# A layer of eight experts: rows gathered by a token list instead of scattered, on one core

## The chip, the cores and the metric

The kernel runs on one core of one Trainium2 chip. The metric is the device time of one execution in microseconds (us), the median of several executions. A profile is one further execution, recorded by the hardware profiler.

## The reference

The program is a chain of eight residual layers on `x`, 16 batches of 128 tokens with 256 features. The change touches the feed-forward layers of blocks 0 and 1; the one it rewrites is block 1's, with eight experts:

```
x = x + _L1_ffn_ref(_layernorm(x, axis=-1), Wr, Wg, Wu, Wd)

router_logits = jnp.einsum('bsh,he->bse', hidden_states, Wr)       # 8 experts
topk_logits, selected = jax.lax.top_k(router_logits, 2)
router_probs = jax.nn.softmax(topk_logits, axis=-1)
for e in range(8):
    w_e = jnp.where(selected == e, router_probs, 0.0).sum(axis=-1, keepdims=True)
    g = jnp.clip(jax.nn.silu(hidden_states @ Wg[e]), -7.0, 7.0)
    u = hidden_states @ Wu[e]
    out = out + ((g * u) @ Wd[e]) * w_e
```

Each of the 2048 tokens goes to two experts, so 4096 rows of 256 numbers have to be brought together by expert, multiplied, and brought back.

## The kernel before

The program is a list of stages with a barrier of all five engines between them. Each stage is written by hand, engine by engine, and its engines wait for each other by semaphores. The stages are attention, the layer of 32 experts (`MoeTop6`), the attention with fp8 weights (`Fp8Attention`), the layer of eight experts (`MoeTop2`), and then attention and feed-forward twice more. X, the activations, stays in SBUF throughout.

`MoeTop2` works in three parts.

**Routing** goes over four groups of four batches. On VectorE (DVE) a group has `moments` (mean and variance), `normalise` (writes `n_xn`), `choose` (top two of the eight logits, one-hot rows `n_hot`, running sums `n_before`) and `slots` (from the counts of TensorE, the place of each of a token's two copies). On TensorE (PE) it has `transposes`, `logits` and `counts`. DVE mixes the groups: moments of group g+2 and choose of group g-1 stand between the normalisations, so group 2 is normalised only after group 0 has been chosen. The place is a row of an array in HBM, `top_in`, with a region of 2048 rows for each expert, 16384 rows in all. GpSimd (POOL) scatters: 32 indirect DMAs (L2151), each of 128 rows of 1 KB, at most eight in flight. `top_in` is set to zero beforehand by eight DMAs of 2 MB each (`clear`, L1776), which SP issues in the middle of the stage before. After the fourth group `layout` works out, for each of the 39 tiles of 128 rows that the experts can fill together, whose expert it is (`n_own`) and which rows of `top_in` it has (`n_row`).

**The expert loop** takes the 39 tiles. POOL gathers a tile's rows (L2161, after all scatters have landed, six tiles ahead), PE transposes them (`rows_T`, L1864), multiplies by Wg and Wu (`up`, L1877), transposes the hidden rows (L1889) and multiplies by Wd (`down`, L1900). SP stores each result tile to `top_out`. `places`, in the second step of the loop on DVE, works out where in `top_out` a token's two rows will be.

**Return**: when all result tiles are stored, POOL gathers two rows for each token (32 indirect DMAs) and DVE adds them to X.

SP loads constants and all expert weights (16 DMAs, 6.3 MB) at the start of the stage, and `up` waits for all of them before the first tile.

`MoeTop6` already has a token list: `places` writes two arrays of ones in bf16, `m_in_tile` (which tile a copy is in, times the token's batch, and times its lane) and `m_at_place` (which of the 128 rows of the tile); PE multiplies one by the other (`tokens`, L1320), which sums up to "the token at each place"; after a transpose `end_tokens` makes `m_token`, and POOL gathers from `moe_in`, the normalised tokens in their own order (L1706). `m_at_place` is made by 24 instructions of 128x128 for each group:

```
for n in range(NG * TOP_K):
    i, j = divmod(n, TOP_K)
    x = v.tensor_scalar(self.at_place[:, i, j, :], self.count16[:, :], self.cutf[:, 1, i, j:j + 1], None, ALU.is_equal)
```

## Time and profile before

| | |
|---|---|
| median of 3 executions | 2559.22 us (2554.13 to 2559.9) |
| profiled execution, its own time | 2561.87 us |
| span of the profiled execution | 2560.1 us |
| mean granted TensorE clock | 0.877 of full |
| PE, DVE, ACT, POOL busy | 2031.7, 1799.2, 1404.7, 1214.1 us |

The span runs from the first to the last instruction. Starts are us from the span's start. In a timeline row the columns are the start, the length, the engine, the line of the kernel, the operation, what it writes and reads, how many instructions are merged, and in brackets how long the engine stood idle before and what ended that. A granted clock of 1.00 is 2.4 GHz, and 0.50 is 1.2 GHz. In a row of windows the pairs are the busy us and the count of PE, PEld (weight loads), DVE, ACT and POOL, followed by the granted clock, the busy share of the DMA engines and GB/s.

### The profile page before, as it was taken

The page shows a single profiled execution, that of the slowest core. Times are in us where ns is not written, and L with a number is a line of the kernel's source. Part 1 is how long each engine was busy: PE and PEld are TensorE (multiplying, and loading weights), DVE is VectorE, ACT ScalarE, POOL GpSimd, SP SyncE. Part 2 cuts the span into 40 slices and gives each one's busy share as a digit, 9 for nine tenths or more (in the row PEclk, how much of TensorE's full clock was granted, in tenths as well). Part 3 has the DMA queues.
Part 4 walks back from the last instruction along what each step waited for, and adds up shares of the span by engine and source line. Part 5 has one row for each costly group of instructions (what it writes and reads, how often), then busy time and mean ns, then how long its engine had stood idle before and what let it go on. Part 6 is the DMA issues. An engine that isn't in the chain of part 4 may idle for free. (4 is left out here: it accounts for less than half of the span.)

```text
span 2560.1 us, 42709 instructions
## 1 busy us (share of the span) xinstructions
PE 2031.7 (79%) x13434; PEld 1241.5 (48%) x13434; DVE 1799.2 (70%) x4099; ACT 1404.7 (55%) x3553; POOL 1214.1 (47%) x1425
## 2 busy tenths in 40 slices
PE   6999699996899999999999539708844536787487
PEld 3444356663577767677777426404412223333144
DVE  4899594755798999999997623338837756888254
ACT  1777322541788888888888403205644422677343
POOL 4443003435788888888876363265412212343100
PEclk9999789997999999999999759857876655999599
DMA  4566305772207000000000222259710015676100
GB/s 134 168 173 170 119 1 156 243 241 62 44 20 284 20 18 20 23 16 20 20 9 1 101 87 88 75 167 237 205 60 1 1 49 145 160 189 176 44 1 33
DMA packets 264488, 242.06 MB, mean 95 GB/s; under 512 B 37002, under 2 KB 236141, under 8 KB 263629
## 3 DMA queue, kind: packets, MB, share of 16 engines
q1 hardware_dynamic: 237996, 187.71, 25.2%
q0 software_dynamic: 13776, 36.59, 5.2%
q10 hardware_dynamic: 12496, 15.03, 1.7%
q8 instruction: 114, 1.87, 0.3%
q14 instruction: 106, 0.86, 0.1%
HBM read 141.95 MB, written 98.19 MB: 94 GB/s over the span
## 5 line engine op out<-in xcount | busy, mean ns | idle before, releaser
L736 DVE TENSOR_REDUCE a_nm<-bank 128x2 f32<-128x512 f32 x640 | 408.8, 683 | 36.8 <-PE bank L602 34.6
L844 ACT ACTIVATE a_PT<-bank 128x512 f32<-128x512 f32 x640 | 355.4, 603 | 142.9 <-PE bank L609 128.1
L602 PE MATMUL bank<-a_stack_k,a_stack_q 48*128 48x256 bf16 (+2 forms) x1280 | 262.1, 298 | 99.1 <-DVE a_nm L736 61.1
L2858 PE MATMUL bank<-f_w,f_zc 128*128 128x512 bf16 x1152 | 283.6, 383 | 22.3 <-DVE f_zc L2966 18.1
L3178 POOL TENSOR_TENSOR f_hr<-f_hr,half_pow 128x4 f32<-128x4 f32 x192 | 245.4, 1278 | 85.2 <-DVE f_hr L2975 85.1
L609 PE MATMUL bank<-a_stack_q,a_stack_k 51*128 51x256 bf16 (+2 forms) x1280 | 251.2, 288 | 7.6 <-ACT a_PT L844 7.1
L3070 ACT ACTIVATE f_Pm<-bank,f_nmax 128x128 f32<-128x128 f32 x512 | 182.5, 382 | 73.6 <-DVE f_nmax L2990 72.9
L602 PEld LDWEIGHTS bank<-a_stack_k,a_stack_q 48*128 48x128 bf16 (+2 forms) x1280 | 91.6, 99 | 261.5 <-DVE a_nm L736 179.5
L624 PE MATMUL bank<-a_PT,a_V 128*32 128x256 f32 x2560 | 186.2, 412 | 1.4 <-ACT a_PT L844 1.4
L2858 PEld LDWEIGHTS bank<-f_w,f_zc 128*128 128x128 bf16 x1152 | 112.5, 99 | 122.5 <-issue 25.8
L3167 POOL TENSOR_TENSOR f_cf<-f_cbr,f_cmr 128x516 f32<-128x516 bf16 x128 | 156.9, 1226 | 12.6 <-DVE f_cb L3015 11.0
L2985 DVE TENSOR_TENSOR f_raw<-bank,f_hr 128x512 f32<-128x512 f32 x192 | 131.5, 685 | 42.9 <-POOL f_hr L3178 42.8
L1706 POOL DMA_INDIRECT m_xe<-moe_in,m_token x64 | 75.8, 1184 | 178.6 <-DVE m_token L1584 93.8
L3082 ACT ACTIVATE f_cb<-bank,f_rsmooth 128x128 bf16<-128x128 f32 x512 | 147.1, 377 | 23.8 <-PE bank L2818 23.8
L2975 DVE TENSOR_REDUCE f_hr<-f_sq 128x4 f32<-128x516 f32 x192 | 131.3, 684 | 39.2 <-ACT f_sq L3105 37.2
L3105 ACT ACTIVATE f_sq<-bank 128x512 f32<-128x512 f32 x192 | 116.5, 607 | 62.7 <-PE bank L2858 39.3
L3172 POOL TENSOR_TENSOR f_Pm<-f_Pm,f_rs 128x512 f32<-128x512 f32 x128 | 132.6, 1036 | 23.3 <-DVE f_rs L2995 23.1
L2807 PEld LDWEIGHTS bank<-f_KT,f_QT 128*128 128x128 f32 x1024 | 129.3, 192 | 20.0 <-issue 10.8
L2807 PE MATMUL bank<-f_KT,f_QT 128*128 128x128 f32 x1024 | 135.2, 275 | 0.0
L2818 PE MATMUL bank<-f_PT,f_Vv 128*128 128x256 f32 x512 | 132.1, 381 | 2.3 <-ACT f_cb L3082 2.3
L930 POOL TENSOR_TENSOR a_rest<-a_QK,a_parts 128x512 f32<-128x512 f32 x48 | 55.7, 1161 | 164.0 <-ACT a_parts L901 164.0
L977 POOL DMA_INDIRECT f_rows<-moe_out,slot x96 | 107.5, 1120 | 46.1 <-ACTq L129 29.8
(365 smaller groups left out, 4804.1 us busy)
## 6 DMA issues: line engine op xcount, KB each, us to landing
cut<-a_parts SPq DMA_DIRECT2D x96, 192.0 KB
cut<-a_parts SPq DMA_DIRECT2D x144, 128.0 KB
o<-a_O SPq DMA_DIRECT2D x32, 512.0 KB, 3.7
top_in<-zero SPq DMA_DIRECT2D x8, 2048.0 KB, 19.4
a_stack_q<-cut SPq DMA_DIRECT2D x64, 192.0 KB
a_stack_k<-cut SPq DMA_DIRECT2D x64, 192.0 KB
m_w<-in_w SPq DMA_DIRECT2D x32, 368.0 KB
moe_out<-m_oe ACTq DMA_DIRECT2D x32, 256.0 KB
```

Source lines behind the costliest of these rows:

```text
L602: x = t.matmul(ps[:, n * D:(n + 1) * D], self.stack_q[rows, i, slot, n * P:(n + 1) * P], self.stack_k[rows, i, slot, :], start=True, stop= ...
L609: x = t.matmul(ps[:, n * D:(n + 1) * D], self.stack_k[rows, i, slot, n * P:(n + 1) * P], self.stack_q[rows, i, slot, :], start=True, stop= ...
L624: x = t.matmul(self.k.bank[6][32 * s:32 * s + 32, half], self.V1[:, b % self.NV, m, first + s, :], self.PT[:, (4 * q + s) % 8, m, :], star ...
L736: v.tensor_reduce(self.nm[:, g % 2, :, at % self.J, at // self.J], self.k.bank[h % 3][:, :].rearrange("p (n m) -> p n m", n=2), AX.X, ALU. ...
L844: a.activation(self.PT[:, h % 8, :, :].rearrange("p m n -> p (m n)"), self.k.bank[3 + h % 3][:, :], ACT.Exp).then_inc(self.a_exp.sem, 1)
L2807: x = t.matmul(ps[:, j * P:(j + 1) * P], self.QT[:, cross, h, :], self.KT[:, cross, h // 2, :], start=True, stop=True)
L2858: x = t.matmul(ps[:, :], self.zc[:, b % 2, j, c_, :], self.fp8.w3[:, m, c_, at:at + BANK], start=(m == 0 and c_ == 0), stop=(m == 2 and c_ ...
L3070: x = a.activation(self.Pm[:, i, j * P:(j + 1) * P], ps[:, j * P:(j + 1) * P], ACT.Exp, bias=self.nmax[:, i, j:j + 1], accum_out=self.rs[: ...
L3082: x = a.activation(self.cb[:, u % self.NCB, j * P:(j + 1) * P], ps[:, j * P:(j + 1) * P], ACT.Copy, scale=self.fp8.rsmooth[:, h:h + 1])
L3167: g.tensor_tensor(self.cf[:, :].rearrange("p (r n) -> p r n", r=3), clipped, steps, ALU.add).then_inc(self.g_c.sem, 1)
L3172: g.tensor_tensor(pm, pm, self.rs[:, u % 3, :].unsqueeze(2).to_broadcast([P, self.HPB, P]), ALU.mult).then_inc(self.g_P.sem, 1)
L3178: g.tensor_tensor(f, f, self.k.half_pow[:, 0:self.HPB], ALU.pow).then_inc(self.g_hr.sem, 1)
```

## The change

`MoeTop2` no longer scatters. The normalised tokens are written to `moe_in` by four plain DMAs. `slots` also writes `n_at_place` for its group; after the fourth group a new function, `list_tokens`, writes `n_in_tile`; PE multiplies (32 products of ones, 78 columns by 128), DVE copies, PE transposes, DVE copies again and makes `n_token`; POOL's 39 gathers take their rows from `moe_in`. `clear`, `top_in`, `n_row` and the 32 scatters are gone. All groups are normalised before the first is chosen. SP stores the tokens between the weights of experts 0 to 3 and those of 4 to 7. In `MoeTop6` the 24 instructions for `m_at_place` become one.

```diff
 class MoeTop6(Stage):            # places()
-        for n in range(NG * TOP_K):
-            i, j = divmod(n, TOP_K)
-            x = v.tensor_scalar(self.at_place[:, i, j, :], self.count16[:, :], self.cutf[:, 1, i, j:j + 1], None, ALU.is_equal)
-            if n < NG * TOP_K - 1:
-                c.mark(x)
-        x.then_inc(self.v_hot.sem, 1)
+        v.tensor_tensor(self.at_place[:, :, :, :], counting(P), self.spread(self.cutf[:, 1, :, :], P), ALU.is_equal).then_inc(self.v_hot.sem, 1)
 class MoeTop2(Stage):            # sp()
-        sp.dma_start(self.tile[:, :, :], A["c_tile"]).then_inc(self.d_par.sem, 16)
+        sp.dma_start(self.count[:, :], A["c_count"]).then_inc(self.d_par.sem, 16)
+        sp.dma_start(self.lane[:, :], A["c_lane"]).then_inc(self.d_par.sem, 16)
+        self.load_experts(sp, range(0, 4))
+        for g in range(self.GROUPS):
+            bs = slice(self.NG * g, self.NG * (g + 1))
+            sp.wait_ge(self.v_n.sem, self.v_n.at(g + 1))
+            sp.dma_start(self.rows_in[:, bs, :], self.xn[:, bs, :]).then_inc(self.d_rows.sem, 16)
+        self.load_experts(sp, range(4, self.NE))
                                  # pe()
-        for g in range(self.GROUPS + 2):
+        for g in range(self.GROUPS + 3):
             if g < self.GROUPS:
                 self.transposes(t, g)
             if 1 <= g <= self.GROUPS:
                 self.logits(t, g - 1)
-            if g >= 2:
-                self.counts(t, g - 2)
+            if g >= 3:
+                self.counts(t, g - 3)
         self.totals(t)
+        self.tokens(t)
+    def tokens(self, t):
+        n, last = 2 * self.NT, 2 * B - 1
+        t.wait_ge(self.v_hot.sem, self.v_hot.at(1))
+        for i in range(2 * B):
+            b, j = divmod(i, 2)
+            x = t.matmul(self.k.bank[7][0:n, 0:P], self.in_tile[:, b, j, :, :].rearrange("p m n -> p (m n)"), self.at_place[:, b, j, :],
+                         start=(i == 0), stop=(i == last))
+        x.then_inc(self.p_who.sem, 1)
+        t.wait_ge(self.v_who.sem, self.v_who.at(1))
+        t.transpose(self.k.bank[6][:, 0:n], self.who[:, :], self.k.ident[0:n, 0:n]).then_inc(self.p_list.sem, 1)
                                  # dve()
-        self.moments(v, 0)
-        self.moments(v, 1)
-        self.constants(v)
-        for g in range(self.GROUPS + 2):
+        for g in range(self.GROUPS + 1):
             if g < self.GROUPS:
-                self.normalise(v, g)
-            if g + 2 < self.GROUPS:
-                self.moments(v, g + 2)
-            if 1 <= g <= self.GROUPS:
-                self.choose(v, g - 1)
-            if g >= 2:
-                self.slots(v, g - 2)
-        self.layout(v)
+                self.moments(v, g)
+            if g == 1:
+                self.constants(v)
+            if g:
+                self.normalise(v, g - 1)
+        for g in range(self.GROUPS + 1):
+            if g < self.GROUPS:
+                self.choose(v, g)
+            if g == self.GROUPS:
+                self.layout(v)
+            if g:
+                self.slots(v, g - 1)
+        self.list_tokens(v)
                                  # slots(), at its end
+        v.wait_ge(self.v_slot.sem, self.v_slot.at(g + 1))
+        c.mark(v.tensor_scalar(self.cut[:, 0, sl, :], self.slot[:, sl, :], 7, None, ALU.logical_shift_right))
+        c.mark(v.tensor_scalar(self.cut[:, 1, sl, :], self.slot[:, sl, :], P - 1, None, ALU.bitwise_and))
+        c.after()
+        c.mark(v.tensor_copy(self.cutf[:, :, sl, :], self.cut[:, :, sl, :]))
+        c.after()
+        c.mark(v.tensor_tensor(self.at_place[:, sl, :, :], self.counting(NG, 2, P), self.spread(self.cutf[:, 1, sl, :], P), ALU.is_equal))
+    def list_tokens(self, v):
+        c.after()
+        self.by_expert(v, slice(0, B), self.tiles[:, 1, :].unsqueeze(1).to_broadcast([P, B, self.NE]))
+        c.mark(v.tensor_tensor(self.cutf[:, 0, :, :], self.cutf[:, 0, :, :], self.slotf[:, :, :], ALU.add))
+        c.after()
+        c.mark(v.tensor_tensor(tile[:, :, :, 0, :], self.counting(B, 2, NT), self.spread(self.cutf[:, 0, :, :], NT), ALU.is_equal))
+        c.after()
+        c.mark(v.tensor_tensor(tile[:, :, :, 1, :], tile[:, :, :, 0, :],
+                               self.spread(self.spread(self.count[:, 0:B], 2), NT), ALU.mult))
+        c.after()
+        v.tensor_scalar(tile[:, :, :, 0, :], tile[:, :, :, 0, :], self.lane[:, 0:1], None, ALU.mult).then_inc(self.v_hot.sem, 1)
+        self.owners(v)
+        v.wait_ge(self.p_who.sem, self.p_who.at(1))
+        v.tensor_copy(self.who[:, :], self.k.bank[7][0:2 * NT, 0:P]).then_inc(self.v_who.sem, 1)
+        v.wait_ge(self.p_list.sem, self.p_list.at(1))
+        v.tensor_copy(self.listed[:, :, :].rearrange("p m n -> p (m n)"), self.k.bank[6][:, 0:2 * NT]).then_inc(self.v_list.sem, 1)
+        v.wait_ge(self.v_list.sem, self.v_list.at(1))
+        v.scalar_tensor_tensor(self.token[:, :], self.listed[:, 1, :], float(P), self.listed[:, 0, :], ALU.mult,
+                               ALU.add).then_inc(self.v_token.sem, 1)
                                  # pool()
-        g.wait_ge(self.d_clear.sem, self.d_clear.at(self.NE))
-        for b in range(B):
-            ...
-                g.indirect_dma_start(self.rows_in, at, self.xn[:, b, :], None, bounds_check=self.NE * self.REGION - 1,
-                                     oob_is_err=False).then_inc(self.d_scat[b % 4].sem, 16)
-        g.wait_ge(self.v_row.sem, self.v_row.at(1))
-        for i in range(4):
-            g.wait_ge(self.d_scat[i].sem, self.d_scat[i].at(2 * (B // 4)))
+        g.wait_ge(self.v_token.sem, self.v_token.at(1))
+        g.wait_ge(self.d_rows.sem, self.d_rows.at(self.GROUPS))
 class Fp8Attention(Stage):       # sp()
-            if b == 4 and self.top2:
-                self.top2.clear(sp)
```

On DVE, from the end of the routing of `MoeTop2`, the kernel before has this (the names are the arrays named above; `n_past` and `n_rowf` lead to `n_row`):

```order
L2018 TENSOR_SCALAR n_tiles<-bank 128x8
L2020 TENSOR_SCALAR n_tiles<-n_tiles 128x8
L2022 TENSOR_TENSOR n_upto<-n_upto,n_tiles 128x64
L2023 TENSOR_SCALAR n_tiles<-n_tiles 128x8
L2025 TENSOR_REDUCE n_incl<-n_upto 128x8
L2027 TENSOR_TENSOR n_past<-n_incl,n_tile 128x273
L2030 TENSOR_REDUCE n_ownf<-n_past 1x39
L2031 TENSOR_TENSOR n_pastw<-n_past,n_tiles 128x273
L2034 CAST n_own<-n_ownf 1x39
L2035 TENSOR_REDUCE n_rowf<-n_pastw 128x39
L2037 TENSOR_TENSOR n_rowf<-n_rowf,n_tile 128x39
L2039 TENSOR_SCALAR n_row<-n_rowf 128x39
```

The changed kernel has, at the same place, from the last instruction of the fourth group's `slots` on (`n_cutf` holds tile and place of each copy as numbers):

```order
L2028 TENSOR_TENSOR n_at_place<-n_count,n_cutf 128x1024
L2008 TENSOR_TENSOR n_hotw<-n_hot,n_tiles 128x16x8 x2
L2010 TENSOR_REDUCE n_slotf<-n_hotw 128x32
L2060 TENSOR_TENSOR n_cutf<-n_cutf,n_slotf 128x32
L2062 TENSOR_TENSOR n_in_tile<-n_count,n_cutf 128x32x39
L2064 TENSOR_TENSOR n_in_tile<-n_in_tile,n_count 128x32x39
L2067 TENSOR_SCALAR n_in_tile<-n_in_tile,n_lane 128x32x39
L2080 TENSOR_TENSOR n_past<-n_incl,n_count 1x273
L2083 TENSOR_REDUCE n_ownf<-n_past 1x39
L2085 CAST n_own<-n_ownf 1x39
L2070 COPY n_who<-bank 78x128
L2074 SCALAR_TENSOR_TENSOR n_token<-n_listed 128x39
```

The owners of the tiles now come after the arrays of ones, and the chain from there to the list runs over PE and back twice (of the last rows, the copy to `n_listed` is left out).

On PE, the routing of `MoeTop2` before, from its first transposes to the total counts:

```order
L1827 MATMUL bank<-ident,n_xn 128x128 x16
L1837 MATMUL bank<-n_wr,n_xnT 128x8 x8
L1827 MATMUL bank<-ident,n_xn 128x128 x8
L1837 MATMUL bank<-n_wr,n_xnT 128x8 x8
L1850 MATMUL bank<-n_before,n_ones 128x32
L1851 MATMUL bank<-n_hit,n_tri 128x32
L1827 MATMUL bank<-ident,n_xn 128x128 x8
L1837 MATMUL bank<-n_wr,n_xnT 128x8 x8
```

And the changed one, over the same work and its new end:

```order
L1833 MATMUL bank<-n_wr,n_xnT 128x8 x8
L1823 MATMUL bank<-ident,n_xn 128x128 x8
L1833 MATMUL bank<-n_wr,n_xnT 128x8 x8
L1846 MATMUL bank<-n_before,n_ones 128x32
L1847 MATMUL bank<-n_hit,n_tri 128x32
L1833 MATMUL bank<-n_wr,n_xnT 128x8 x8
```

The first counts (`n_before`, `n_hit`) moved behind the last transposes, that is, one group later than before.

## Rows read from the trace of the kernel before

**Rows 1.** Timeline of POOL in `MoeTop2`: first scatter, last scatter, first gather

```profile
1474.72 1.07 POOL L2151 DMA_INDIRECT top_in<-n_xn,n_slot  x1 [16.52 <-DVE n_slot L2011]
...
1515.80 0.97 POOL L2151 DMA_INDIRECT top_in<-n_xn,n_slot  x1 [0.30 <-DMA top_in<-n_xn,n_slot]
1519.05 1.04 POOL L2161 DMA_INDIRECT n_xe<-top_in,n_row  x1 [2.28 <-DMA top_in<-n_xn,n_slot]
```

**Rows 2.** Windows in `MoeTop2`: two of the routing, one of the expert loop

```profile
1460.00:1465.00 5.00, 0.66 (x3) 0.56 (x4) 3.94 (x26) 0.20 (x1) 0.00 (x0) 0.50 1.01 391
1465.00:1470.00 5.00, 5.00 (x26) 4.90 (x25) 0.03 (x1) 1.17 (x2) 0.00 (x0) 0.50 0.01 4
...
1600.00:1640.00 40.00, 40.00 (x161) 24.87 (x160) 13.96 (x41) 13.79 (x41) 6.98 (x7) 1.00 0.23 70
```

**Rows 3.** Timeline of DVE at the start of `MoeTop2`

```profile
1445.78 1.41 DVE L1934 BATCH_NORM_STATS2 n_stats<-X 128x6 f32<-128x256 f32 x4 [5.35 <-POOLq L129]
...
1450.08 0.23 DVE L1946 CAST n_tri<-n_trif 128x128 bf16<-128x128 f32 x1 [0.35 <-DMA n_tile<-in_c_tile]
...
1450.58 1.38 DVE L1957 TENSOR_SCALAR n_xn<-X,n_mv,n_rstd 128x256 f32<-128x256 f32 x4
...
1453.80 1.38 DVE L1957 TENSOR_SCALAR n_xn<-X,n_mv,n_rstd 128x256 f32<-128x256 f32 x4
```

**Rows 4.** Timeline of PE: transposes of group 1, logits of group 0

```profile
1455.23 1.97 PE L1827 MATMUL bank<-ident,n_xn 128*128 128x128 f32 x8 [1.19 <-DVE n_xn L1957]
...
1456.99 3.42 PE L1837 MATMUL bank<-n_wr,n_xnT 128*128 128x8 f32 x16
```

**Rows 5.** Timeline of DVE: `choose` of group 1, `slots` of group 0, next

```profile
1469.97 0.19 DVE L1969 COPY n_lg<-bank 128x32 f32<-128x32 f32 x1 [5.28 <-PE bank L1837]
...
1472.84 0.19 DVE L2007 TENSOR_TENSOR n_where<-bank,n_region 128x32 f32<-128x32 f32 x1
...
1473.72 1.38 DVE L1957 TENSOR_SCALAR n_xn<-X,n_mv,n_rstd 128x256 f32<-128x256 f32 x4
```

**Rows 6.** Timeline of DVE in `MoeTop6`: the arrays of ones, fourth group

```profile
384.19 1.76 DVE L1555 TENSOR_TENSOR m_in_tile<-m_count,m_cutf 128x1536 bf16<-128x1536 f32 x1
...
386.79 0.62 DVE L1560 TENSOR_SCALAR m_in_tile<-m_in_tile,m_lane 128x1536 bf16<-128x1536 bf16 x1
387.32 3.99 DVE L1563 TENSOR_SCALAR m_at_place<-m_count,m_cutf 128x128 bf16<-128x128 bf16 x24
```

**Rows 7.** Timeline of DVE in the expert loop: `places` over all batches

```profile
1530.16 0.49 DVE L1999 TENSOR_TENSOR n_hotw<-n_hot,n_where 128x128 f32<-128x128 f32 x2
...
1530.69 0.42 DVE L2001 TENSOR_REDUCE n_slotf<-n_hotw 128x32 f32<-128x256 f32 x1
```

**Rows 8.** Timeline of `MoeTop6`: products of ones, token list, first gather

```profile
394.89 1.50 PE L1320 MATMUL bank<-m_at_place,m_in_tile 128*128 128x128 bf16 x24
...
400.87 0.23 DVE L1584 SCALAR_TENSOR_TENSOR m_token<-m_who 128x64 uint32<-128x64 f32 x1
402.00 1.22 POOL L1706 DMA_INDIRECT m_xe<-moe_in,m_token  x1 [93.78 <-DVE m_token L1584]
```

**Rows 9.** Timeline of PE at the start of the expert loop

```profile
1521.98 0.66 PE L1864 MATMUL bank<-ident,n_xe 128*128 128x128 f32 x2 [32.03 <-issue]
...
1524.34 3.78 PE L1877 MATMUL bank<-n_wgu,n_xeT 128*128 x4 [0.39 <-issue]
```

**Rows 10.** Instructions of `clear`: min/median/max ns, first and last start

```profile
L1776 SPq DMA_DIRECT2D top_in<-zero x8: 592/4989/5706, 785.6 to 812.4; - x8
```

**Rows 11.** Timeline of ACT in `Fp8Attention`: one copy in each batch

```profile
776.45 0.41 ACT L3055 COPY f_zT<-bank 128x256 f32<-128x256 f32 x1
...
826.49 0.42 ACT L3055 COPY f_zT<-bank 128x256 f32<-128x256 f32 x1
...
876.52 0.41 ACT L3055 COPY f_zT<-bank 128x256 f32<-128x256 f32 x1
```

**Rows 12.** Waits of PE in `MoeTop6`'s routing: us, times, longest

```profile
PE bank L1302 <- DVE m_hit L1516: 4.8, 3, 1.8
```

More of the change, by code:

```diff
@@ L1753, in signals @@
         claim, G, NT = self.k.sig.claim, self.GROUPS, self.NT
-        self.d_par, self.d_w = claim("d_par", 4, 16), claim("n_d_w", 2 * self.NE, 16)
-        self.d_scat = [claim(f"n_d_scat{i}", B // 4 * 2, 16, own=True) for i in range(4)]
+        self.d_par, self.d_w = claim("d_par", 5, 16), claim("n_d_w", 2 * self.NE, 16)
+        self.d_rows = claim("n_d_rows", G, 16)
         self.d_xe = [claim(f"n_d_xe{i}", -(-(NT - i) // self.RX), 16, own=True) for i in range(self.RX)]
@@ L1767, in signals @@
         self.v_sum = claim("n_v_sum", B)
-    def clear(self, sp):
-        k, n = self.k, 8
-        rows = self.rows_in.rearrange("(e p n r) d -> e p n (r d)", e=self.NE, p=P, n=n)
-        for e in range(self.NE):
-            sp.dma_start(rows[e], k.zero[:, :].unsqueeze(1).to_broadcast([P, n, FILL])).then_inc(self.d_clear.sem, 16)
     def sp(self, sp):
@@ L2022, in layout @@
         c.mark(v.tensor_tensor(self.upto[:, :, :], self.upto[:, :, :], n.unsqueeze(1).to_broadcast([P, NE, NE]), ALU.mult))
-        c.mark(v.tensor_scalar(tiles[:, 1, :], n, -float(P), float(self.REGION), ALU.mult, ALU.add))
         c.after()
@@ L2026, in layout @@
         c.after()
-        c.mark(v.tensor_tensor(self.past[:, :, :], self.incl[:, 0:NE - 1].unsqueeze(1).to_broadcast([P, NT, NE - 1]),
-                               self.tile[:, 0, :].unsqueeze(2).to_broadcast([P, NT, NE - 1]), ALU.is_le))
+        c.mark(v.tensor_tensor(before, self.incl[:, :], n, ALU.subtract))
+    def list_tokens(self, v):
+        c, NT, tile = self.k.dve, self.NT, self.in_tile
+        flat = lambda a: a.rearrange("p b j -> p (b j)")
         c.after()
-        c.mark(v.tensor_reduce(self.ownf[:, :], self.past[0:1, :, :], AX.X, ALU.add))
@@ L2033, in layout @@
         c.after()
         v.tensor_copy(self.own[:, :], self.ownf[:, :]).then_inc(self.v_own.sem, 1)
-        c.mark(v.tensor_reduce(self.rowf[:, :], self.pastw[:, :, :], AX.X, ALU.add))
-        c.after()
-        c.mark(v.tensor_tensor(self.rowf[:, :], self.rowf[:, :], self.tile[:, 1, :], ALU.add))
-        c.after()
-        v.tensor_scalar(self.row[:, :], self.rowf[:, :], float(NE * self.REGION - 1), None, ALU.min).then_inc(self.v_row.sem, 1)
-    def places(self, v):
-        c, NE, pr = self.k.dve, self.NE, self.pr
-        before = self.tiles[:, 2, :]
-        c.mark(v.tensor_tensor(before, self.incl[:, :], self.tiles[:, 0, :], ALU.subtract))
-        c.after()
-        c.mark(v.scalar_tensor_tensor(before, before, float(P), self.region[:, 0, :], ALU.mult, ALU.subtract))
-        c.after()
-        c.mark(v.tensor_scalar(before, before, -1.0, None, ALU.add))
-        c.after()
-        c.mark(v.tensor_tensor(self.where[:, :, :], self.where[:, :, :], before.unsqueeze(1).to_broadcast([P, B, NE]), ALU.add))
-        c.after()
-        self.by_expert(v, slice(0, B), self.where[:, :, :])
-        v.tensor_copy(self.place[:, :, :], self.slotf[:, :, :]).then_inc(self.v_place.sem, 1)
@@ L2055, in places @@
+    def places(self, v):
+        c, pr = self.k.dve, self.pr
+        v.scalar_tensor_tensor(self.place[:, :, :], self.cutf[:, 0, :, :], float(P), self.cutf[:, 1, :, :], ALU.mult,
+                               ALU.add).then_inc(self.v_place.sem, 1)
         v.wait_ge(self.a_df.sem, self.a_df.at(self.GROUPS))
@@ L3195, in program @@
             stage(Attention(k, 0, None))
-        top2 = MoeTop2(k, 1 not in stages) if 3 in stages else None
         if 1 in stages:
@@ L3202, in program @@
                 stage(MoeTop6(k, combine, fp8))
-                stage(Fp8Attention(k, combine, fp8, top2))
+                stage(Fp8Attention(k, combine, fp8))
         if 3 in stages:
-            stage(top2)
+            stage(MoeTop2(k))
         if 4 in stages:
```

90 lines of the change are left out of this document (46 added, 44 removed).

## The prediction

> **What bounds the kernel now.** The change lies in three stages, so I read those stages and not the whole. First the timeline of POOL in the stage of eight experts. Its scatters run from 1474.72 to 1515.80 us, 32 of them, 1.33 us apart, each about 1.0 us of work for POOL; the first gather starts at 1519.05, held at the end by the landing of the last scatter [rows 1]. Then the windows: in the routing TensorE's granted clock is 0.50 even where it is busy for 5.00 of 5.00 us; in the expert loop TensorE is busy for 40.00 of 40.00 us at full clock, so the loop is TensorE's own time [rows 2]. From this, everything between the start of the stage (1445.78) and the first gather (1519.05) is time in which the loop waits, 73.3 us, and for the last 44.3 of them it is POOL alone that counts. What the change is worth is the start of the first gather, before against after. The timelines of VectorE and TensorE in the routing give the pieces for that [rows 3 to 5]. The list itself is shown by its twin, the layer of 32 experts, in timelines [rows 6, 8].
>
> **The new path to the first gather.** I walk it from 1445.78, with the durations of the kernel before.
>
> *Normalisation.* Two moments, a wait for constants and the small constants take 4.80 us, to 1450.58 [rows 3]. There was a wait of 0.35 us for the last constant. Now one more tiny constant is issued behind a slightly larger one; I add 0.4 us, bounded by 0 and 1. The first normalisation starts at 1451.0. A normalisation and a moment together took 3.22 us (1450.58 to 1453.80) [rows 3], so the second starts at 1454.2. The last two groups follow by about 1460.2; they are hidden, since TensorE is now behind.
>
> *TensorE.* Its transposes of group 1 started 1.43 us after the normalisation of that group did, and the logits of group 0 ended 5.18 us after those transposes started (1455.23 to 1456.99 + 3.42) [rows 4]. So now: transposes at 1455.6, logits 0 done at 1460.8, and with 5.18 us for each further pair of transposes and logits, logits 1 at 1466.0 and logits 2 at 1471.2. The first counts stand behind these and are done at 1471.5. This is the price of normalising all groups first: the first place is known later. Nothing waits for it alone any more.
>
> *VectorE.* One `choose` is 2.87 us (1469.97 to 1472.84), one `slots` 0.88 us (1472.84 to 1473.72) [rows 5]. `slots` grows by two cuts and a cast (0.5 us) and by the array of ones, 1024 elements. The twin writes 1536 elements of the same form in 1.76 us [rows 6]; with about 0.16 us that do not scale, 1024 are 1.23 us. A `slots` is then 2.65 us. Chooses 0 and 1 are done while TensorE works on; from 1471.5 VectorE alone sets the pace: four `slots` (10.6), two `choose` (5.7), the shortened `layout` (five small instructions, 1.0): 1488.8.
>
> *List.* `n_hotw` and its reduction over all batches took 0.98 us with their waits (0.49 and 0.42 busy) [rows 7], the sum 0.2. Two arrays of 1248 elements at the twin's rate are 1.46 each, 3.0 with the waits; the last, single-source one is 0.55 (0.62 for 1536 elements [rows 6]). Together 4.8 us: 1493.6. TensorE's 32 products follow: 24 took 1.50 us [rows 8] at full clock, so 2.0, and at half clock 4.0. The clock stood at 0.50 in this routing [rows 2]; I take 4.0. The owners of the tiles are made meanwhile. Copy, transpose, copy: 1.3 us, sized by the small instructions around. The token instruction starts at 1499.0, and the twin's first gather started 1.13 us after it (400.87 to 402.00) [rows 8]. First gather: 1500.2.
>
> That is **18.9 us** earlier than 1519.05. I round the path up by 0.3 for gaps that I haven't counted: 18.6.
>
> **What else moves.** *Expert weights.* Half of them now wait on SP behind the four stores of tokens, which wait for the normalisations, so they go out from about 1460.2. With the stores (2.1 MB) 5.2 MB remain; at the 391 GB/s of [rows 2] that takes 13.4 us, to 1474. The first tile needs them near 1503, so they cost nothing; that cover ends only below 121 GB/s. Before, the queue was empty again from 1465 on (4 GB/s) [rows 2]. The stores have landed long before the gather that needs them.
>
> *The clearing.* Its eight DMAs run from 785.6 to 812.4 [rows 10]. The batch of the fp8 attention in which they fall lasts 50.04 us (776.45 to 826.49), the next one, without them, 50.03 [rows 11]. So taking them away gains nothing.
>
> *The layer of 32 experts.* 24 instructions, 3.99 us, become one of 3072 elements: by the row of 1536 that is 1.60 x 2 + 0.16 = 3.36 us, 0.63 less [rows 6]. TensorE waits for VectorE's `m_hit` three times, the longest 1.8 us [rows 12]; two of these waits have a `places` ahead of them in VectorE's order (those of groups 1 and 2); the `places` of groups 0 and 3 lie where TensorE is behind. So twice 0.63, 1.3 us with the dropped cast, bounds 0 and 4.7 (a re-rise of the clock after each wait could go too, about 1.7 us each, by the 3.78 against half of it for the same four products in [rows 9]). Here the Trainium skill speaks against the change: "VectorE: DVE Perf Modes", section "The TRN2 errata", gives a fixed 58 cycles and one element a cycle for an instruction with two tensors, four for a single-source one in bf16. By its figures 24 small ones would be 2.25 us (an estimate) and the big one 3.26, a loss of 1.0 for each group and 2.0 on the path; this trace has 3.99 for the 24, so it doesn't agree.
>
> *The rest.* The expert loop has the same products, the 32 gathers at the end and their places are the same, the later stages are untouched.
>
> **Sum.** 2561.87 (the profiled execution's own time) - 18.6 - 1.3 = 2542.0. The median of the timed runs is 2.65 below the profiled one, so the prediction is **2539.3 us**, 0.78% less.
>
> **The rivals.**
> - *The clock rises in the routing (faster than forecast).* TensorE is now busy without a gap from 1455.6 to 1471.5, and it could be granted 2.4 GHz; the pairs of 5.18 us would shrink, until VectorE sets the pace from about 1465.9 (end of the last normalisation plus two `choose`), and the products of ones would take 2.0: up to 7.6 us, 2532. Against it: the window with 5.00 of 5.00 busy at 0.50 [rows 2]. A smaller form of it is the start of the loop, where the first products took 3.78 us, cold [rows 9]; up to 3 us less if the products of ones warm the array. Chance 12%. The Trainium skill, "TensorE: Matmul & The Clock Gate", section "What's actually happening", says that a busy array is passed every clock pulse; by that rule alone this rival would be the forecast, and the trace of this routing doesn't bear it out.
> - *The chain is longer (smaller gain).* VectorE, TensorE, VectorE, TensorE, VectorE, POOL hand over to each other, and each gap may be larger; or the constants are late. Twice my allowances is 5 us: 2544. Chance 10%.
> - *The weights are late.* Below 121 GB/s `up` would wait. At 80 GB/s they would land at 1525 and all is lost again: 2558, no change. Against it: 391 GB/s [rows 2]. 2%.
> - *The gathers are slow (slower than before).* Rows now lie scattered in `moe_in`, and all of the 896 empty places (39 x 128 - 4096) read the same row, where a tile used to read consecutive rows. The loop turns in about 3.06 us (40 us for some 13 tiles) [rows 2]. If a gather took more than that, all 39 would hold the loop: at 3.54 us the gain is gone, at 3.8 the kernel is 10 us slower, 2568. For it: nothing in the trace shows such a gather with many equal rows. Against it: the twin gathers from the same array. 3%.
> - *No gain to see* for a reason I don't know, 3%.
>
> **How the numbers follow.** The forecast itself has 70%; its own terms give 2535 to 2544: the clock in the products of ones (-2), the constants (-0.4 to +0.6), `MoeTop6` (-3.4 to +1.3), gaps (+2), and the repetition of the median (its three runs lie 5.8 us apart). The range takes in most of the first two rivals: 2532 to 2546. A measurement of this kernel can tell about 0.3%, 7.7 us, from no change. Faster takes the forecast, the first two rivals and a part of the last: 0.94; no change 0.03; slower 0.03.
>
> **What the changed kernel's profile would show.** First gather near 1499 (that is 1500.2 less the 1.3 us of the earlier stage), right behind `n_token`; first counts near 1470; VectorE dense from there to about 1492; 32 products in 4 us at clock 0.50; TensorE waiting for no weights; the batches of the fp8 attention still 50.04 us; loop and return as long as before. I am wrong if the first gather stands after 1504 or before 1495, or if the loop has become longer than before.

## The result, and the profile after

The changed kernel takes **2530.9 us** (median of 4 executions, 2527.77 to 2534.57), the kernel before 2557.16 us beside it on the same chip (2554.13 to 2559.9). The ratio is 0.9898, interval 0.9876 to 0.9920, which is 26.1 us less (26.3 by the two medians), between 20.5 and 31.7. The prediction was 2539.3, range 2532 to 2546: the direction is right, the gain is larger than the range allows, by 1.1 us. The profiled execution of the changed kernel took 2534.57 us, with a span of 2532.8 and a mean granted clock of 0.883.

DVE at the start of `MoeTop2` (answers to [rows 3]; columns as there):

```profile
1449.22 1.41 DVE L1944 BATCH_NORM_STATS2 n_stats<-X 128x6 f32<-128x256 f32 x4 [5.35 <-POOLq L129]
...
1453.09 0.23 DVE L1956 CAST n_tri<-n_trif 128x128 bf16<-128x128 f32 x1
...
1453.52 1.37 DVE L1966 TENSOR_SCALAR n_xn<-X,n_mv,n_rstd 128x256 f32<-128x256 f32 x4
```

All times of the routing are best read from the stage's first instruction, 1449.22 now and 1445.78 before. The wait for constants has gone altogether: the first normalisation starts 4.30 us into the stage, where it was 4.80 us.

PE from the second transposes to the loop (answers to [rows 4, 8 and 9]):

```profile
1458.16 1.97 PE L1823 MATMUL bank<-ident,n_xn 128*128 128x128 f32 x8 [1.19 <-DVE n_xn L1966]
1459.92 3.42 PE L1833 MATMUL bank<-n_wr,n_xnT 128*128 128x8 f32 x16
1463.20 1.95 PE L1823 MATMUL bank<-ident,n_xn 128*128 128x128 f32 x8
1464.94 3.42 PE L1833 MATMUL bank<-n_wr,n_xnT 128*128 128x8 f32 x16
1468.21 1.95 PE L1823 MATMUL bank<-ident,n_xn 128*128 128x128 f32 x8
1469.95 3.42 PE L1833 MATMUL bank<-n_wr,n_xnT 128*128 128x8 f32 x16
1473.22 0.19 PE L1846 MATMUL bank<-n_before,n_ones 128*128 128x32 bf16 x1
...
1495.76 3.63 PE L1858 MATMUL bank<-n_at_place,n_in_tile 128*78 128x128 bf16 x32 [10.95 <-DVE n_in_tile L2067]
1499.77 0.39 PE L1862 MATMUL bank<-ident,n_who 78*128 78x78 f32 x1 [0.38 <-DVE n_who L2070]
1504.40 0.66 PE L1872 MATMUL bank<-ident,n_xe 128*128 128x128 f32 x2 [4.23 <-issue]
```

TensorE now works without a gap from 1458.16 through the counts of the first two groups, to 1476.91; from there it waits for VectorE, the last time for 10.95 us. VectorE over the same stretch (answers to [rows 5 to 8]):

```profile
1473.55 0.19 DVE L2017 TENSOR_SCALAR n_where<-bank 128x32 f32<-128x32 f32 x1 [2.25 <-PE bank L1847]
...
1475.05 1.23 DVE L2028 TENSOR_TENSOR n_at_place<-n_count,n_cutf 128x1024 bf16<-128x1024 f32 x1
1476.19 0.18 DVE L1978 COPY n_lg<-bank 128x32 f32<-128x32 f32 x1
...
1492.15 1.46 DVE L2062 TENSOR_TENSOR n_in_tile<-n_count,n_cutf 128x1248 bf16<-128x1248 f32 x1
1493.65 1.46 DVE L2064 TENSOR_TENSOR n_in_tile<-n_in_tile,n_count 128x1248 bf16<-128x1248 bf16 x1
1495.14 0.56 DVE L2067 TENSOR_SCALAR n_in_tile<-n_in_tile,n_lane 128x1248 bf16<-128x1248 bf16 x1
...
1500.47 0.20 DVE L2074 SCALAR_TENSOR_TENSOR n_token<-n_listed 128x39 uint32<-128x39 f32 x1
```

Between 1473.55 and 1495.70 VectorE has no idle time in brackets: it is the bound of this stretch. The gather follows. POOL's timeline (the first line answers to [rows 1]; the last two are the end of the stage and its barrier):

```profile
1501.46 1.09 POOL L2187 DMA_INDIRECT n_xe<-moe_in,n_token  x1 [40.10 <-DVE n_token L2074]
...
1670.66 1.00 POOL L2198 DMA_INDIRECT n_rows<-top_out,n_place  x1 [0.30 <-issue]
1677.61 0.52 POOL L906 MEMSET a_V<- 128x512 f32 x1 [5.96 <-POOLq L129]
```

The first gather comes 52.2 us into the stage, where it was 73.3. The last line is one that I had not looked at before: POOL's first instruction of the next stage, with 5.96 us from the last gather to it, and `POOLq L129`, POOL's own drain and barrier, as what it waited for. In POOL's timeline of the kernel before the same place reads:

```profile
1689.19 1.00 POOL L2172 DMA_INDIRECT n_rows<-top_out,n_place  x1 [0.31 <-issue]
1698.76 0.52 POOL L908 MEMSET a_V<- 128x512 f32 x1 [8.57 <-POOLq L129]
```

VectorE's last addition ends 2.8 us after that gather does, in both. Behind it VectorE waits for POOL; its first instruction of the next stage, in the kernel before and then in the changed one:

```profile
1698.76 0.27 DVE L698 MEMSET a_one<- 3x256 bf16 x1 [5.75 <-POOLq L129]
```

```profile
1677.61 0.27 DVE L696 MEMSET a_one<- 3x256 bf16 x1 [3.15 <-POOLq L129]
```

How the gain runs through the program, by the first (or last) start of an instruction in each of the two profiles (the differences are taken before rounding):

| from ... to | before | after | |
|---|---|---|---|
| start to `m_stats` (attention 0) | 297.7 | 303.8 | +6.2 |
| to `m_token` (routing of `MoeTop6`) | 103.2 | 100.4 | -2.8 |
| to `n_stats` (experts, fp8 attention) | 1044.9 | 1044.9 | 0 |
| to first `n_xe` gather (routing of `MoeTop2`) | 73.3 | 52.2 | -21.0 |
| to first `n_rows` gather (expert loop) | 129.5 | 128.8 | -0.7 |
| to last `n_rows` gather (return) | 40.6 | 40.4 | -0.2 |
| to `b_stats` (barrier, attention 2) | 206.3 | 203.3 | -2.9 |
| to last `a_stats` (block 2's feed-forward, most of attention 3) | 433.2 | 431.7 | -1.6 |
| to `t_stats` (end of attention 3) | 81.1 | 77.2 | -3.9 |
| to the end | 150.3 | 150.0 | -0.3 |

Steps that contain no changed instruction moved by up to 6 us too; in this pair their shifts nearly cancel. How much of each shift is the change could not be told from one pair, and that is what most of the experiments are for.

### The profile page after: what moved, and what is told of

It is laid out like the page before. It is cut to its first block and busy times, and to the rows that moved or that the text cites. A ratio compares the mean times of both kernels' runs of the same rounds, so it can differ in the third digit from the quotient of the medians.

```text
span 2532.8 us, 42624 instructions
## 1 busy us (share of the span) xinstructions
PE 2033.0 (80%) x13467; PEld 1245.5 (49%) x13467; DVE 1807.1 (71%) x4020; ACT 1404.6 (55%) x3553; POOL 1182.0 (47%) x1393
```

## The experiments

Each run leaves a profile too, so every kernel is one more sample of all the stages that it doesn't touch. "Stage" below is the time from `n_stats` to the first gather.

**Theory A**: the gain is what the two changed places give, and the rest is variation between executions. **Rival B**: removing 16 MB of `top_in` and its clearing made later stages faster.

### The list without the one large instruction

```diff
 # MoeTop6.places()
-        v.tensor_tensor(self.at_place[:, :, :, :], counting(P), self.spread(self.cutf[:, 1, :, :], P), ALU.is_equal)...
+        for n in range(NG * TOP_K):
+            ...
+            x = v.tensor_scalar(self.at_place[:, i, j, :], self.count16[:, :], self.cutf[:, 1, i, j:j + 1], None, ALU.is_equal)
```

> The changed kernel with the 24 small instructions for m_at_place put back in MoeTop6; everything else as changed. Theory A (what the change saves lies in two places: 21.0 us from the start of the eight-expert stage to its first gather, and about 2.7 us in the routing of MoeTop6; the few us by which untouched attention stages moved, +6.1 and about -9, are a variation between executions): from the start of MoeTop2 to its first gather 52.2 us as in the changed kernel; m_stats to m_token back at 103.2 us from 100.5; gain over the kernel before 21 to 23 us in the median. Rival B (the stages behind MoeTop2 really became faster because 16 MB of top_in, and its clearing, are gone): a_stats to t_stats and the step before b_stats are shorter than in the kernel before by 3 to 4 us each here too.

Measured: 2532.14 us against 2559.42, ratio 0.9898 (0.9877 to 0.9919). The stage is 52.4 us, as theory A has it. `m_stats` to `m_token` is 105.1, not less than the 103.2 expected, and the gain in the median is 27.3 us where 21 to 23 was expected: the number was missed, and without the large instruction the kernel is not measurably slower. Rival B isn't settled here: the steps that it names are 202.5 (to `b_stats`) and 77.2 us (to `t_stats`), shorter than before by as much as it says.

### The one large instruction alone

```diff
 # the kernel before, MoeTop6.places()
-        for n in range(NG * TOP_K): ...
+        v.tensor_tensor(self.at_place[:, :, :, :], counting(P), self.spread(self.cutf[:, 1, :, :], P), ALU.is_equal)...
```

> The kernel before with only the one large instruction for m_at_place in MoeTop6. By the prediction's term it gains 1.3 us; by what the changed kernel's trace suggests 2.7, because TensorE's granted clock does not fall after its second wait for m_hit: in the trace m_stats to m_token would be 100.5 us, not 103.2 (or 101.9 if only the durations count). The median can hardly tell either from nothing. Rival C (a loss: one element after another in one large instruction is slower than 24 small ones): 105 us. Theory A also expects here, in attention stages whose code is that of the kernel before, shifts of several us of either sign against the first profile.

Measured: 2557.4 us (12 executions) against 2559.42 (17), ratio 1.0000 (0.9988 to 1.0013). `m_stats` to `m_token` is 100.5. Rival C's 105 us stands in none of the twelve profiles with the large instruction: they give that step as 100.4 or 100.5 three times and 102.3 to 103.5 nine times (mean 102.4). The two without it have 103.2 and 105.1, a difference of 1.8 us on average; but 103.2 lies among the nine, so from two profiles the size can't be told. Where the 2.8 of the first pair has its luck, the windows show. In the three short ones (the changed kernel, this one, and the one with 32 gathers below) TensorE's granted clock stays at 1.00 from 345 us to the list; in the nine others it falls to 0.50 for some 3 to 7 us about TensorE's last wait for `m_hit`, and the list comes 13.5 us after the start of the last array and not 12.2.

This run also answers the question on the untouched stages. Behind `m_token` it is the kernel before, instruction for instruction, yet its `m_stats` stands at 305.2 (the kernel before: 297.7) and its last `a_stats` to `t_stats` is 77.0 (the kernel before: 81.1). Over all fourteen profiles `m_stats` lies between 296.8 and 305.4, and that last step between 75.8 and 81.1, on both sides of the change. Theory A holds for them. This run also has 72.3 us from `n_stats` to the first gather, with the routing of the kernel before, whose profile has 73.3: a stage can differ by 1 us without a change.

### The clearing kept

```diff
 # Fp8Attention.sp()
+            if b == 4 and self.top2:
+                self.top2.clear(sp)          # 8 x 2 MB into an array that nobody reads
 # MoeTop2.pool()
+        g.wait_ge(self.d_clear.sem, self.d_clear.at(self.NE))
```

> The changed kernel with the 16 MB array in HBM and its eight clearing DMAs in the middle of the fp8 attention kept (nothing reads the array; the gathers wait for the clearing too). Theory A: same time as the changed kernel within its scatter, 2528 to 2534, and batches of the fp8 attention of 50.04 us with and without the clearing; a step from MoeTop2's last add to b_stats and from a_stats to t_stats that varies as in the others. Rival B: those two steps go back to the lengths before (202.9 and 81.1 us), about 7 us slower, 2536 to 2540.

Measured: 2529.87 us against 2559.42, ratio 0.9885 (0.9865 to 0.9906), so not slower than the changed kernel; last `n_rows` to `b_stats` is 200.5, shorter than in the changed kernel, and last `a_stats` to `t_stats` 80.1, which two kernels without the clearing have as well (80.4 and 80.2). Rival B is refuted, and the prediction's zero for the clearing stands.

### The old order of the groups, with the list

```diff
 # MoeTop2.dve(); PE's counts of group g-2 likewise
-        for g in range(self.GROUPS + 1): moments(g); normalise(g - 1)
-        for g in range(self.GROUPS + 1): choose(g); slots(g - 1)
+        for g in range(self.GROUPS + 2): normalise(g); moments(g + 2); choose(g - 1); slots(g - 2)
```

> The changed kernel with the groups mixed on VectorE as before (normalisation of group g, moments of g+2, choice of g-1, slots of g-2) and counts of group g-2 on TensorE; the token list is kept. Theory A (the order is worth something because TensorE at half clock would otherwise wait for each normalisation): last choice near 41 + 2 us after the start of the stage, then two slots, layout and the list: first gather 60 to 64 us after the stage's start against 52.2, 8 to 11 us slower than the changed kernel. Rival D (the order is worth nothing, the list alone brings the gain, since VectorE's sum of work is the same): 52 to 54 us.

Measured: 2537.93 us against 2559.42, ratio 0.9914 (0.9892 to 0.9935). Stage 61.0, as theory A has it; rival D is refuted. The median is 7.0 us above that of the changed kernel. VectorE's timeline shows where it goes, the start of `choose` for the second and third groups:

```profile
1472.77 0.19 DVE L1978 COPY n_lg<-bank 128x32 f32<-128x32 f32 x1 [5.27 <-PE bank L1833]
...
1484.92 0.19 DVE L1978 COPY n_lg<-bank 128x32 f32<-128x32 f32 x1 [5.27 <-PE bank L1833]
```

Each time a group's normalisation stands behind the `choose` of an earlier group, TensorE gets it late and VectorE then waits 5.27 us for the logits. With the 3.34 us in front of the first `choose` these waits add up to 13.9 us. With all groups normalised first there are three of 0.60, 2.25 and 2.25 us (in front of the first and second `choose` and the first `slots`), 5.1 together: that is the 8.8 us less. Of the 21.0 us of the stage, the order with its later counts is 8.7 and the list 12.3 (73.3 to 61.0).

### Three edits to the new routing

First, counts of a group one step earlier on TensorE:

```diff
 # MoeTop2.pe()
-            if g >= 3:
-                self.counts(t, g - 3)
+            if g >= 2:
+                self.counts(t, g - 2)
```

> The changed kernel with one edit on TensorE: the counts of group g stand right behind the logits of group g+1 and not of g+2. The prediction said that VectorE alone sets the pace from the first counts on, and VectorE idles 2.25 us in front of the first place computation. Theory A: this idle time goes, first gather 50.0 us after the start of the stage against 52.3, 2.3 us faster. Rival: TensorE then waits for VectorE's choice and its transposes of group 3 and logits come later: no gain, 52.3.

Measured: 2526.54 us against 2558.87, ratio 0.9882 (0.9860 to 0.9904). Stage 50.0: the idle time of 2.25 us in front of the first `slots` is gone. The first counts did have something waiting for them alone, and the new order doesn't need them late: with the counts where the old order has them, the order is worth 11.0 us (61.0 to 50.0).

Second, the last array in two halves:

```diff
 # MoeTop2.list_tokens()
-        (three instructions on n_in_tile, all 16 batches)
+        for h in range(2):
+            bs = slice(h * B // 2, (h + 1) * B // 2)
+            (the same three on batches bs)  ... .then_inc(self.v_hot.sem, 1)
```

> The changed kernel with n_in_tile written for batches 0 to 7 first and 8 to 15 behind, and the 32 products of ones begun after the first half. The 32 products took 3.63 us with the clock at 0.50, all behind the last instruction on n_in_tile. If they cost their full length on the path, half of them (1.8 us) now lies beside VectorE's second half, less 0.4 us for three more small instructions: first gather 50.9 us after the stage's start against 52.3. If the products slow VectorE down or wait for something else, 52.3 or more.

PE begins its products after the first half. Measured: 2532.91 us against 2558.87, ratio 0.9889 (0.9869 to 0.9909). Stage 50.9, as expected; VectorE's wait for the products falls from 2.72 to 0.97 us.

Third, TensorE is kept busy while it waits, with products whose result nobody reads:

```diff
 # MoeTop2.pe()
         self.totals(t)
+        self.idle_products(t, 20)
         self.tokens(t)
+        self.idle_products(t, 8)
```

> The changed kernel with idle products (128x512, bf16, result unused) on TensorE: 20 of them while it waits for the list (where it stood idle for 10.95 us), 8 while it waits for the first gather. If the granted clock follows what TensorE does, the products of ones run at 1.00 in 1.8 us and not 3.63, and the loop starts at full clock, where it now runs at 0.50 for some 9.6 us (1504.40 to about 1514): 4 to 6 us faster in all. Rival: the clock stays at 0.50 in the routing whatever TensorE does (it did where it was busy for 5.00 of 5.00 us), no gain, or a loss of 1 us where the idle products stand in the way.

Measured: 2529.09 us against 2558.87, ratio 0.9897 (0.9866 to 0.9929). Stage 51.8 us, loop 129.5. The granted clock in windows over the idle products, the gap behind them, the products of ones and the loop's start (last three figures: granted clock, DMA share, GB/s):

```profile
1479.00:1482.00 3.00, 3.00 (x9) 1.07 (x8) 2.73 (x10) 0.00 (x0) 0.00 (x0) 0.50 0.00 0
1482.00:1485.00 3.00, 2.80 (x13) 1.07 (x11) 2.75 (x11) 0.00 (x0) 0.00 (x0) 0.98 0.00 0
1485.00:1488.00 3.00, 0.00 (x0) 0.00 (x0) 2.86 (x6) 0.00 (x0) 0.00 (x0) 1.00 0.00 0
1488.00:1491.00 3.00, 1.34 (x13) 1.34 (x14) 2.51 (x5) 0.00 (x0) 0.00 (x0) 0.66 0.00 0
1491.00:1494.00 3.00, 2.62 (x26) 2.19 (x25) 0.62 (x3) 0.00 (x0) 0.00 (x0) 0.77 0.00 0
...
1500.00:1503.00 3.00, 2.73 (x4) 1.19 (x5) 0.00 (x0) 1.54 (x2) 2.19 (x3) 0.50 0.31 87
```

Neither side was right as it stood. The clock does rise with what TensorE does (0.98 at the end of the idle products), so 0.50 is no law of this routing. But the idle products were then done (at 1484.8, 4.9 us before the last array of ones was), the clock fell again just before the products of ones began (0.50 from 1489; 3.26 us for them, not 1.8), and at the loop's first `up` it was back at 0.50. So 0.5 us was gained in the stage and 0.7 given back in the loop, whose clock came back 11 us after the first gather and not 10 (windows of 1 us: 1506 after 1494.90, in the changed kernel 1511 after 1501.46). That also says that the expected 4 to 6 us were too many: the loop of the changed kernel ran at 0.50 until 1511, 6.7 us from its first transposes, not 9.6. A longer row of idle products was not tried.

### What the barrier costs

Scatters put back, beside the loop:

```diff
 # MoeTop2.pool(), behind the gather of tile j, n = j - 6, n = 0 to 31
+                at = bass.IndirectOffsetOnAxis(ap=self.place[:, n // 2, n % 2:n % 2 + 1], axis=0)
+                g.indirect_dma_start(self.spare, at, self.xn[:, n // 2, :], None, ...)
```

> The changed kernel with 32 indirect scatters more: POOL writes the normalised rows into an array that nobody reads, one behind each of the gathers 6 to 37, beside the expert loop. It asks about the barrier behind MoeTop2: POOL needed 8.57 us from its last gather to the next stage in both kernels with scatters and 5.96 us in all four with the list (VectorE waited 5.75 and 3.15 us for it). Theory E (the drain of POOL costs more after more indirect DMAs or after scatters): 8.57 us again here. Rival F (it is about where POOL's program lies, or what is gone from the stages before): 5.96 or another number. It also says whether scatters are dear by themselves: the loop is TensorE's own time, so 128.7 us from first gather to first return gather if they are free beside it.

Measured: 2531.57 us against 2558.87, ratio 0.9903 (0.9877 to 0.9929). The loop is 128.7, the barrier:

```profile
1679.62 0.52 POOL L906 MEMSET a_V<- 128x512 f32 x1 [8.57 <-POOLq L129]
```

8.57 us, the number of the kernel before to the hundredth, as theory E has it, and VectorE's wait is 5.74. The median can't show these 2.6 us: it is 0.7 above that of the changed kernel, and its four executions lie 11 us apart. Three more kernels, with a single execution each, ask what exactly is counted. POOL with 96 small instructions more:

```diff
+        for n in range(96):
+            g.memset(self.idle[:, n, :], 0.0)
```

> The changed kernel with 96 tiny memsets more on POOL, while POOL waits for the list. Asks about the barrier behind MoeTop2, which cost 5.96 us with the list and 8.57 us when 32 scatters were put back beside the loop. If the number of POOL's instructions in the stage counts: about 8.6 or more. If it is the indirect DMAs: 5.96.

32 gathers in place of the 32 scatters:

```diff
-                g.indirect_dma_start(self.spare, at, self.xn[:, n // 2, :], None, ...)
+                g.indirect_dma_start(self.unused[:, n % 4, :], None, self.k.xbuf, at, ...)
```

> The changed kernel with 32 more indirect gathers beside the loop (into a tile that nobody reads), where the earlier run had 32 scatters. If the barrier grows with the number of indirect DMAs of either kind: 8.57 us. If only scatters (rows written to HBM by POOL) make it dearer: 5.96.

16 scatters in place of 32:

```diff
-            if 0 <= n < 2 * B:
+            if 0 <= n < B:
```

> The changed kernel with 16 more scatters beside the loop, half of those of the earlier run. If the barrier grows by a fixed price for each indirect DMA (2.61 us for 32, 0.082 each): 7.27 us. If it is a step (one scatter is enough, or a threshold): 5.96 or 8.57.

POOL's first instruction behind the barrier, small instructions:

```profile
1672.82 0.53 POOL L906 MEMSET a_V<- 128x512 f32 x1 [5.96 <-POOLq L129]
```

32 gathers:

```profile
1689.24 0.53 POOL L906 MEMSET a_V<- 128x512 f32 x1 [8.57 <-POOLq L129]
```

16 scatters:

```profile
1685.06 0.53 POOL L906 MEMSET a_V<- 128x512 f32 x1 [7.26 <-POOLq L129]
```

So it is the number of indirect DMAs that the stage has issued on POOL, scatters and gathers alike: 71 give 5.96, 87 give 7.26, 103 give 8.57, which is 0.082 us each, and by that line some 0.17 us would be left for none (5.96 - 71 x 0.0816, an estimate). The traces bear that out: in the stages that issue no indirect DMA, POOL's drain ends 0.07 to 0.08 us after POOL's last work. POOL's other instructions don't count. Each of these DMAs moves 128 rows, so a price for each row can't be told from a price for each DMA.

The three times were 2526.68, 2539.64 and 2539.91 us. In the last two the loop took 136.1 and 134.1 us, where 32 scatters left it at 128.7; PE's waits there add up to about 4 us more, 2.4 of them in one place. Why they did and the 32 scatters didn't stays open; more DMAs alone is no explanation, since 16 of them were slower than 32.

### Both edits to the routing together

> The changed kernel with both edits that shortened the routing: counts one group earlier (2.3 us) and n_in_tile in two halves (1.4 us). They lie one behind the other on the path, so they should add: first gather 48.6 us after the stage's start against 52.3, and 3.7 us less than the changed kernel in all. If one hid what the other takes away: 49.5 to 50.0.

Measured: 2528.53 us (5 executions) against 2557.95, ratio 0.9886 (0.9865 to 0.9906). Stage 48.8: the two edits add (2.2 and 1.3 alone, 3.4 together). This is the shortest stage of all the kernels, and its profiled execution, 2525.56 us, is the lowest of the profiled ones. The medians can't tell it from the changed kernel.

## Why the prediction was right in direction and short in size

Against 2539.3 the measured median is 8.4 us lower. Of that, 2.1 is luck of the measurement: the median of the kernel before was 2557.2 beside the changed kernel and not 2559.2. The rest is in four places. None of them shows in the prediction's own signs of being wrong: counted from the stage's start in the kernel before, less the 1.3 us, the first gather stands at 1496.7, between 1495 and 1504, and the loop didn't become longer. For the largest term that it left out it had no sign.

- **The step that failed: "loop and return as long as before", and with it the sum's silence about what follows the return.** The barrier behind `MoeTop2` became 2.6 us shorter. It had been visible: in the kernel before, VectorE waited 5.75 us for POOL at a place that I hadn't looked at because nothing in it was changed. The removed scatters were charged with their own time (about 1.0 us each for POOL), not with what POOL's drain asks for each of them at the end. Four experiments show the drain's length and what it depends on. That VectorE's next work starts 2.6 us earlier is in the rows; how much of it reaches the end of the program is argued from them, since later steps vary by more.
- **The loop** became 0.7 us shorter in the first pair; no experiment separates this term. In the kernel before, the old `places`, eleven instructions from 1529.23 to 1531.91 in the middle of which stand [rows 7], held back `n_h` of the second tile: ScalarE had its input ready at 1530.64, and VectorE's timeline goes on from the last of the eleven with

```profile
1531.73 0.18 DVE L2060 TENSOR_TENSOR n_pr<-n_pr 128x16 f32<-128x16 f32 x1
1531.94 0.29 DVE L2067 TENSOR_SCALAR n_sg<-n_sg 128x256 f32<-128x256 f32 x1
```

  PE's timeline has an idle time ahead of the transposes of that tile's hidden rows there, and none in the changed kernel:

```profile
1532.74 0.44 PE L1889 MATMUL bank<-ident,n_h 128*128 128x128 f32 x2 [0.36 <-issue]
```

```profile
1514.93 0.38 PE L1897 MATMUL bank<-ident,n_h 128*128 128x128 f32 x2
```

  The diff leaves four of the eleven; the prediction had "the 32 gathers at the end and their places are the same" and costed nothing. The kernels with the list have loops of 128.1 to 129.1 us (129.5 with idle products), without the two slow ones. The run of the large instruction alone, with the old `places`, has 130.5, but that isn't a second witness: there PE waits 1.40 us at these transposes, and VectorE, done with `places` at 1532.72, itself waits for ScalarE:

```profile
1534.10 0.29 DVE L2062 TENSOR_SCALAR n_sg<-n_sg 128x256 f32<-128x256 f32 x1 [1.38 <-ACT n_sg L2123]
```

  What held ScalarE up is open. Its routing was 1.0 us shorter and its loop 1.0 longer than in the kernel before. So the two steps together are surer than each alone: 202.8 us in both kernels with scatters, 181.0 in the changed one, 21.7 less.
- **The routing**, "18.9 us": the mechanism, the order and every station were right, the size was 21.0. The constants were not 0.4 us later but earlier (0.9 off). A further pair of transposes and logits is 5.02 us and not 5.18, since it follows without a gap. With both, the first counts came 1.4 us before my time. VectorE's stretch from there was 22.1 us, as worked out. The products of ones took 3.63 and not 4.0, the hand-overs behind them were some 0.5 shorter than my allowances, and the 0.3 "for gaps that I haven't counted" wasn't needed. "Nothing waits for it alone any more", of the first counts, was wrong (2.25 us, by the experiment with earlier counts), but the sum had let VectorE start behind them anyway. All errors of this step have one sign: I padded each estimate, and then padded the sum.
- **`MoeTop6`**: 1.3 predicted, 1.8 on average over the profiles, too few to tell the two apart; the new instruction takes 3.35 us against 3.36 worked out. TensorE's two waits behind a `places`, by its timeline in the kernel before,

```profile
356.36 0.19 PE L1302 MATMUL bank<-m_hit,m_ones 128*128 128x32 bf16 x1 [1.80 <-DVE m_hit L1516]
...
377.28 0.19 PE L1302 MATMUL bank<-m_hit,m_ones 128*128 128x32 bf16 x1 [1.80 <-DVE m_hit L1516]
```

  and in the changed kernel:

```profile
362.15 0.19 PE L1300 MATMUL bank<-m_hit,m_ones 128*128 128x32 bf16 x1 [1.17 <-DVE m_hit L1513]
...
382.38 0.19 PE L1300 MATMUL bank<-m_hit,m_ones 128*128 128x32 bf16 x1 [2.81 <-DVE m_hit L1513]
```

  The first is shorter by the 0.63 forecast. The second is longer: behind the first wait the granted clock fell to 0.50 before (358 to 361) and stays at 1.00 now, so TensorE is earlier at the second. So the clock, which the prediction had as a bound and not in the sum, does count: where it doesn't fall at the last wait, the list comes 1.4 us sooner. (The bound's 1.7 us for each re-rise is 1.9 by its own row, half of 3.78.) The Trainium skill ("VectorE: DVE Perf Modes", "The TRN2 errata") would give 3.26 us for the large instruction by its fixed 58 cycles, and 3.36 by the 151 cycles that the same section gives for float32 sums of two tensors (both estimates); the trace has 3.35. Its 58 cycles don't fit the 24 small ones (2.25 against 3.99), which that section says of its row too: it calls it too low for single instructions. With that the loss that the prediction drew from it is refuted.

What was right: the clearing at zero (fp8 batches of 50.03 and 50.04 us in the changed kernel too, of 50.05 and 50.02 with the clearing kept); the weights, whose transfers end soon after 1475, far ahead of the first tile, in the windows of the changed kernel that answer to [rows 2]:

```profile
1470.00:1475.00 5.00, 5.00 (x28) 5.00 (x27) 2.40 (x15) 1.00 (x3) 0.00 (x0) 0.50 1.03 405
1475.00:1480.00 5.00, 2.14 (x13) 1.93 (x13) 4.55 (x29) 0.20 (x1) 0.00 (x0) 0.50 0.10 36
```

The rival of slow gathers with 896 equal rows didn't happen: PE waits for a gather once, 0.7 us, at the second tile, where it was 0.6 before. The rival of the clock rising in the routing by itself didn't either: TensorE was busy for 5.00 of 5.00 us and the clock stood at 0.50 (first of the two rows). By the Trainium skill, "TensorE: Matmul & The Clock Gate", "What's actually happening", a busy array gets every pulse; the rows of the idle products agree with that, the rows of transposes and 8-column logits don't.

The sum as it should have been: 21.7 for the routing and the loop, 2.6 for the barrier, 1.3 to 1.8 for `MoeTop6`, together 25.6 to 26.1, where 26.1 was measured, between 20.5 and 31.7. That it meets so well is luck.

## What to carry to other kernels

When instructions are removed, ask also what the end of the stage charges for them: a drain that follows many indirect DMAs of one engine can be on the path although none of them is. When a diff shortens something "off the path", find the row that waits for it before writing zero. And a pair of profiles can't say whether a stage that wasn't touched became faster: here one such stage spread over 8.6 us between executions, and only further kernels with the same code in that stage showed it. When a wait is named as a cause, look at what the waited-for engine itself was waiting for.

## What the hardware showed that was not expected

- POOL's drain at the barrier behind `MoeTop2` takes 0.082 us for each indirect DMA (128 rows) that the stage has issued: 5.96, 7.26 and 8.57 us for 71, 87 and 103. It goes on for 3.15 to 5.75 us after all of them have landed and VectorE has added the last rows.
- The fp8 attention has 96 indirect DMAs, the last of them issued at 1285.4 of the kernel before, 150 us ahead of its barrier, and POOL's last work there ends at 1437.2; its drain ends 8.6 us later, and the next stage starts at 1445.78. So the price seems to fall due at the drain however long ago the DMAs were; this one was not tried by an experiment. The line of `MoeTop2` would give 7.9 for 96 (an estimate), and for the 64 of `MoeTop6` 5.3, where the drain ends 6.2 us after the last gather in the kernel before and 5.5 in the changed one. So the line is not the whole story in other stages.
- In the kernel before, VectorE's chains of small instructions show idle times of 0.72, 0.39 and 0.93 us between 1484 and 1494, each behind VectorE's own previous instruction, while POOL's scatters run; in the changed kernel, with no scatters there, the same chains have none. What in a scatter holds them up was not tried.
